# A four-layer cross-attention chain: new orders on all engines, work taken from VectorE, layer 3's maximum subtracted by VectorE, and the first feed-forward products split into three F32R products

## The reference, cut to what matters

```
L0: q,k,v = x@Wq+bq, ctx@Wk+bk, ctx@Wv+bv      16 heads of 8; causal mask (key < query), row 0 gives 0
    x = LN(x + softmax(q k^T/sqrt 8) v @ Wo + bo);  x = LN(x + relu(x@W1+b1)@W2 + b2)
L1: same attention without mask or LN;           x = x + gelu(x@W1+b1)@W2 + b2
L2: vis = mean(ctx)@Wv^T+bv; t = x@Wt^T+bt; agreement = sum(t*vis)
    r = softmax over the 64 tokens of 2*agreement
    gate = sigmoid(t@Wgt^T + (r*vis)@Wgv^T + bg);  x = LN(x + gate*r*vis)*gamma + beta
L3: n = x*rsqrt(mean x^2 + eps)*norm_w; q,k,v = n@wq, ctx@wk, ctx@wv    16 heads of 64
    out = x + softmax(q k^T) v @ wo
```

## Time and profile before

| | us |
|---|---|
| median of 3 runs | 1492.05 (1490.93 to 1493.82) |
| the profiled execution | 1493.37 |
| its span, first to last instruction | 1491.8 |
| mean granted TensorE clock, share of full speed | 0.993 |
| PE busy | 1399.8 (94%) |
| PEld busy | 1031.9 (69%) |
| DVE busy | 1074.7 (72%) |
| ACT busy | 955.0 (64%) |
| POOL busy | 504.2 (34%) |

### The profile page before, as it was taken

How to read it: one execution, slowest core, us unless ns; L and a number is a source line. 1 busy time by engine, 2 the same in 40 slices (tenths; PEclk the granted TensorE clock), 3 DMA queues, 4 the chain that set the end, 5 groups by cost and what they waited for, 6 DMA issues and landing times.

```text
span 1491.8 us, 48987 instructions
## 1 busy us (share of the span) xinstructions
PE 1399.8 (94%) x20359; PEld 1031.9 (69%) x20359; DVE 1074.7 (72%) x2647; ACT 955.0 (64%) x1879; POOL 504.2 (34%) x539
## 2 busy tenths in 40 slices
PE   5689999999999999999999999999999999999887
PEld 4356767767676676767767776776767767686666
DVE  6467778676776867778676777867678686776743
ACT  4365657576666756767576676757667676666645
POOL 3141524224251332514224251432425233251412
PEclk9899999999999999999999999999999999999999
DMA  4000000000000000000000000000000000000000
GB/s 144 15 2 2 17 9 17 9 16 10 2 17 9 17 9 2 17 9 17 9 16 10 1 18 8 17 9 8 18 1 17 9 16 10 1 10 2 2 9 9
DMA packets 27799, 20.03 MB, mean 13 GB/s; under 512 B 1088, under 2 KB 27200, under 8 KB 27328
## 3 DMA queue, kind: packets, MB, share of 16 engines
q1 hardware_dynamic: 27584, 16.90, 3.9%
HBM read 12.70 MB, written 4.19 MB: 11 GB/s over the span
## 4 chain that ended last, share of the span: by engine, by line
PE 79%; ACT 7%; DVE 6%; POOL 4%; issue 4%; DMA 0%; SPq 0%; POOLq 0%; DVEq 0%; ACTq 0%
PE bank L751 65%; PE bank L760 14%; ACT V L1114 2%; POOL prob L1202 2%; ACT prob L1132 2%; POOL prob L1182 1%; ACT K L1109 1%; DVE sums L1465 1%; DVE negmax L1311 1%; DVE z L1376 1%; POOL rstd L1189 0%; ACT probT L1064 0%; ACT room L1091 0%; DVE stats L1361 0%; DVE sums L1316 0%
## 5 line engine op out<-in xcount | busy, mean ns | idle before, releaser
L1182 POOL TENSOR_TENSOR prob<-prob,rinv 128x512 f32<-128x512 f32 x256 | 262.0, 1047 | 357.3 <-DVE rinv L1318 357.1
L760 PE MATMUL bank<-cst,prob 128*128 128x128 f32 x1536 | 213.7, 277 | 15.1 <-POOL prob L1182 7.1
L760 PEld LDWEIGHTS bank<-cst,prob 128*128 128x128 f32 x1536 | 174.3, 141 | 66.3 <-issue 37.5
L1202 POOL TENSOR_TENSOR prob<-prob,rinv 128x512 f32<-128x512 f32 x128 | 132.0, 1042 | 199.5 <-DVE rinv L1469 199.5
L1311 DVE TENSOR_REDUCE negmax<-bank 128x8 bf16<-128x512 f32 x256 | 161.3, 681 | 41.8 <-PE bank L751 41.1
L1064 ACT ACTIVATE probT<-bank 128x512 f32<-128x512 f32 x256 | 138.5, 599 | 75.0 <-PE bank L760 74.7
L1057 ACT ACTIVATE prob<-bank 128x512 f32<-128x512 f32 x256 | 141.0, 612 | 70.1 <-PE bank L751 70.0
L1316 DVE TENSOR_REDUCE sums<-prob 128x8 f32<-128x512 f32 x256 | 167.3, 653 | 17.8 <-ACT prob L1057 16.9
L1186 POOL TENSOR_TENSOR var_eps<-mv,ln_eps 128x4 f32<-128x4 f32 x48 | 15.1, 314 | 384.3 <-DVE mv L1366 384.3
L1132 ACT ACTIVATE prob<-bank,rms_rows 128x256 f32<-128x256 f32 x256 | 102.7, 481 | 46.4 <-PE bank L751 46.4
L751 PE MATMUL bank<-negmax,ident_b 128*128 128x512 bf16 x384 | 124.3, 383 | 6.4 <-DVE negmax L1311 5.1
(11 more groups left out here) (168 smaller groups left out, 2952.1 us busy)
## 6 DMA issues: line engine op xcount, KB each, us to landing
x_in<-in_x SPq DMA_DIRECT2D x16, 256.0 KB, 3.0
c_in<-in_ctx SPq DMA_DIRECT2D x16, 256.0 KB, 3.8
out<-y SPq DMA_DIRECT2D x16, 256.0 KB, 2.3
Q<-in_split_weights SPq DMA_DIRECT2D x1, 1536.0 KB, 8.4
wt<-in_weights SPq DMA_DIRECT2D x1, 1024.0 KB, 10.6
wt<-in_weights SPq DMA_DIRECT2D x1, 640.0 KB, 5.4
wt<-in_weights SPq DMA_DIRECT2D x4, 128.0 KB, 10.4
cst<-in_constants SPq DMA_DIRECT2D x1, 229.0 KB, 2.7
```

Of the source, the lines that this page charges most:

```text
L760: last = nc.tensor.transpose(o[:, k * P:(k + 1) * P], src(k), ident)
L1182: nc.gpsimd.tensor_tensor(pr, pr, ri, ALU.mult).then_inc(norm_ready.sem, 1)
L1202: nc.gpsimd.tensor_tensor(pr, pr, ri, ALU.mult).then_inc(norm3_ready.sem, 1)
```

## The change

1. `h` products: W1 of both layers moves from the F32 weights to the split ones, and `h.l.j` becomes three F32R products. Two steps a group and layer are new: `xhi` (ScalarE writes the high half `h_high`, for layer 0 from the bank of `lnF.0` once more, for layer 1 from `x2T`) and `xlo` (GpSimd, `h_low` = value minus high half). The h products wait for `xlo`.
2. Layer 3's shift: `shift3` on TensorE is gone. `sub3.m.e` on VectorE adds the negated maxima to the bank and writes the result to `prob3` in SBUF. `exp3` reads and writes `prob3` in place. The bank is free after `sub3`. The maxima are kept in F32.
3. VectorE's other work: `km` goes to ScalarE as two activations. `vm` copies 256 elements of each partition instead of multiplying 512 by a mask (the zeros are written once at the start). `agree` is gone: `ag` becomes eight products of 64 tokens, whose weights are the sequence's `gv` column repeated 128 times.
4. All four tables, the banks and `TURN` are new, with `km`, `xhi`, `xlo` and `sub3` in their places. `TURN` goes from 89.4057 to 90.4543. It only sets how the lists of the groups are merged.
5. Some waits are joined (`O` waits once for the latest `probT`, `S3.0` for all K3 and Q3 at once). The high and low halves of W1 are made at the start, one activation and one subtraction of 128x1024 more.

```diff
-SPLIT = {"Wk0": 0, "Wk1": 128, "wk3": 256, "wv3": 1280, "wq3": 2304}
+SPLIT = {"Wk0": 0, "Wk1": 128, "wk3": 256, "wv3": 1280, "wq3": 2304, "W1_0": 3328, "W1_1": 3840}
...
-TURN = 89.4057
+TURN = 90.4543
...
-            "S3": lambda g, m, e: exp3_ready(g, m, e), "PT3": lambda g, m, h: prob3T_ready(g, m, h),
+            "S3": lambda g, m, e: shifted3(g, m, e), "PT3": lambda g, m, h: prob3T_ready(g, m, h),
...
-                    pe.wait_ge(*(ln_out(g, 0) if l == 0 else attout_ready(g, 1)))
-                    mm(bank(g, "h", l, j)[:, :], w(f"W1_{l}", j * P), (x1T[0] if l == 0 else x2T)[:, :])\
+                    pe.wait_ge(*h_low_ready(g, l))
+                    split_mm(bank(g, "h", l, j)[:, :], w_split(f"W1_{l}", j * P), (h_high[:, :], h_low[:, :]))\
...
-                    mm(bank(g, "ag")[:, :], ones[:, :], agree_in).then_inc(ag_filled.sem, 1)
+                    for b in range(GB):
+                        rows = slice(b * L, b * L + L)
+                        last = mm(bank(g, "ag")[:, rows], gv[:, cg, 1, b:b + 1].broadcast_to([P, P]), x1T[1][:, rows],
+                                  start=(b == 0))
...
-                elif kind == "shift3":
-                    pe.wait_ge(*max3_ready(g, m, e))
-                    mm(bank(g, "S3", m, e)[:, :], ident_b[:, :],
-                       negmax3[:, m % 2, e, :].unsqueeze(2).broadcast_to([P, 8, L]), start=False)\
...
+                elif kind == "km":
+                    act.wait_ge(*k_filled(g, l))
...
+                    for k in range(2):
+                        last = nc.scalar.activation(Km[l][:, :, k, :], bank(g, "k", l)[:, :].rearrange("p (b k) -> p b k", b=GB),
+                                                    ACT.Identity, bias=bkm[:, l, k:k + 1], scale=m_c2[:, k:k + 1])
...
+                elif kind == "xhi":
+                    if l == 0:
+                        act.wait_ge(*lnF_filled(g, 0))
+                        nc.scalar.activation(h_high[:, :], bank(g, "lnF", 0)[:, :], ACT.Identity, bias=v("ln1_b"),
+                                             scale=v("ln1_g")).then_inc(h_high_ready.sem, 1)
+                    else:
+                        act.wait_ge(*attout_ready(g, 1))
+                        nc.scalar.activation(h_high[:, :], x2T[:, :], ACT.Identity).then_inc(h_high_ready.sem, 1)
...
+                        own = prob3[:, m % 2, :, i, :].rearrange("p (t e) k -> p t e k", e=2)[:, :, e, :]
+                        last = nc.scalar.activation(own, own, ACT.Exp, scale=rms_rows[:, 2 * m + i:2 * m + i + 1])
...
+                elif kind == "xlo":
+                    nc.gpsimd.tensor_tensor(h_low[:, :], (x1T[0] if l == 0 else x2T)[:, :], h_high[:, :], ALU.subtract)\
...
+                        last = nc.vector.tensor_copy(own[:, :, :, k, :], both[:, :, :, k, :])
...
+                elif kind == "sub3":
+                    dve.wait_ge(*max3_ready(g, m, e))
+                    own = prob3[:, m % 2].rearrange("p (t e) i k -> p e i t k", e=2)[:, e]
+                    nc.vector.tensor_tensor(own, bank(g, "S3", m, e)[:, :].rearrange("p (i t k) -> p i t k", i=2, t=4),
+                                            negmax3[:, m % 2, e, :].rearrange("p (i t) -> p i t", i=2).unsqueeze(3)
+                                            .broadcast_to([P, 2, 4, L]), ALU.add).then_inc(shifted3.sem, 1)
```

698 lines of the change are left out of this document (362 added, 336 removed).

## The result

The changed kernel takes 1526.15 us, the median of its runs (1524.46 to 1527.98), against 1492.05: a ratio of 1.023, with a 95% interval of 1.0209 to 1.0251. The forecast was 1510 with a range to 1526. The direction was right. The forecast loss was about half of the measured one (18 of 34 us), and the time lies 0.15 us above the upper end of the range.

The account below looks back on a forecast made before the run. TensorE was taken as the bound, with waits on trips through other engines. Per group -2.1 issue, +2.8 opening, +0.7 before h.0.0 gave +1.4, discounted to 15 us; plus 3 at the end: 1510 us, range 1464 to 1526.

Parts of the forecast that it names:

- The issue time: TensorE's issue per group: h products -1.2 us, layer 3 shifts -1.8, ag +0.9, in sum -2.1.
- Rival (d): By the busy table, split h products add 0.3 us each, 38 us in all: 1530 or more; chance 1%.
- The bounds of the sum: Bounds on TensorE's summed issue change over 16 groups, put at -34 us: -59 to -26.
- The way to `h.0.0`: Layer 1's first h product waits for xlo on GpSimd: +0.7 us a group (0.4 to 1.4).
- Rival (c): GpSimd's xlo, blocked by VectorE, ends up to 0.68 us later: another 0.7 a group, +11 us, 1521; chance 13%.
- The opening after: Opening of layer 3 in the changed kernel: S3.3 starts 13.3 us after the end of S3.0, against 11.85 before.
- The end of layer 3: Last group's layer 3 has nothing beside it, each pair one or two sub3 longer: +3 us.
- The conversion of W1: At the start, converting W1 falls where TensorE waits for transfers anyway: 0 to +3 us.
- I take 0.9 to 1.0, 15 us: Loss per group, cut from the summed +1.4 because some waits elsewhere would disappear; 15 us in all.
- the opening, +2.8 of waiting: Opening of layer 3: TensorE waits 4.7 us against 1.9, +2.8 a group (bounds +1.2 to +3.5).
- The place of the wait: In layer 3's opening, TensorE waits 2.6 us before PT3.0.0, with S.1.0 laid beside the trip as 1.0 us.
- the sign that was to show the forecast right: TensorE's wait for norm3 before PT3.0.0 and PT3.0.1 grows from some tenths to 2 to 3 us a group.

Follow-up runs that it names:

- e4: Changed kernel with the h products as single F32 products again, without xhi, xlo and the W1 conversion; 1532.3 us, ratio 1.0284.
- e1: Changed kernel with xT of group 1 moved on TensorE from fifth step to just before cT of group 1; 1516.7 us, ratio 1.017.
- e7: Changed kernel with group 1's xT and cT later on TensorE, its xT later on VectorE, two GpSimd weight subtractions behind norms; 1518.7 us, ratio 1.0183.
- e10: e7 with three weight conversions on ScalarE behind km.0 instead of qm.0, and VectorE's xT.0 ahead of c_low.0; 1513.0 us, ratio 1.0144.
- e2: Changed kernel with the next group's exp.0.0.0 moved on ScalarE ahead of the exponentials of layer 3's first pair; 1544.2 us, ratio 1.0359.
- e8: e7 with, in the last group, k3.6 and k3.7 later on TensorE and yn_low ahead of y_gamma and y_beta on VectorE; 1519.3 us, ratio 1.0187.
- e5: Kernel before with only sub3 on VectorE in place of shift3, behind each pair of maxima; 1549.4 us, ratio 1.0386.
- e9: Kernel before with only km moved from VectorE to ScalarE; 1536.6 us, ratio 1.0306.
- e11: e10 with layer 3's opening reordered in groups 2 to 11: shift.0.0.0 and its exponential earlier, qm.1 later; 1529.0 us, ratio 1.026.

## Why the prediction was wrong

**Read right.**
- The issue time. One split h product takes 0.70 from start to start (0.71 forecast), one `ag` step 1.83 (1.76), one `sub3` 0.56 to 0.60 where two follow each other, with 0.66 a record (0.64). Busy time would have said the contrary, and e4 confirms the sign: the split of h gains 6 to 8 us. Rival (d) is out. The bounds of the sum, -59 to -26, do not follow from those of its terms, which give -66 to -30; nothing hung on it.
- The way to `h.0.0`: 0.53 of waiting at `q.0` and 0.15 at `h.0.0`, together the 0.7 forecast. But the 0.53 is a wait for VectorE's `xT`, at a step to which the forecast gave no wait, and it is there without the split too (e4). GpSimd's rows in group 11:

```profile
1037.38 1.01 POOL L1244 TENSOR_TENSOR rstd<-var_eps,half 128x4 f32<-128x4 f32 x1
1038.42 1.29 POOL L1236 TENSOR_TENSOR h_low<-x1T,h_high 128x512 fp32r<-128x512 f32 x1
```

- Rival (c), an `xlo` blocked by VectorE, did not happen. It takes 1281 ns on average for layer 0 and 1273 for layer 1, about as long as an `xb`. But this does not test the rule behind the rival, because its condition hardly arose: 31 of the 32 `xlo` have beside them only VectorE instructions that read a bank. The one that meets an instruction on two SBUF tiles began first, and then VectorE was the one that lost: `y_beta` took 1.77 us where the fifteen others took about 0.69.

```profile
1395.00 1.77 DVE L1471 TENSOR_TENSOR y<-y,beta 128x512 f32<-128x512 f32 x1
1394.92 1.30 POOL L1236 TENSOR_TENSOR h_low<-x1T,h_high 128x512 fp32r<-128x512 f32 x1 [2.23 <-ACT h_high L1115]
```

  The Trainium skill, "SBUF — State Buffer", section "SBUF: two separate sides", says that GpSimd and VectorE share a port pair as an exclusive lock: an instruction that begins first holds it to its end, on VectorE's side one in a two-port mode or one with two SBUF inputs, the latter only against a GpSimd instruction that reads SBUF. These two rows agree with it.
- The opening after: forecast 13.3 from the end of `S3.0`, 14.4 with `S3.0` itself, measured 14.54 to 14.61 in the groups without a fall of the clock. The links agree as well: in group 10, counted from 1056.54, `PT3.0.0` starts at 6.7 (6.4 forecast), `PT3.0.1` at 8.1 (7.8) and `S3.3` at 13.4 (13.3).
- The end of layer 3: +3, as forecast.

**The steps that failed.**
1. "The conversion of W1 falls in the start, where TensorE waits for transfers anyway: 0 to +3." It was +17, half of the whole loss and the largest error of the sum; with 0 to 3 in its place the time would have lain inside the range. The sentence looked at the work that was added and not at the order in which the start was now written. For that work alone it was right: e4, without the conversion, has its first `S.0.0` 2.4 earlier. The list of TensorE's first steps showed `xT` of group 1 in fifth place, and that step needs a load that waits for `xb.0`, which waits for GpSimd's subtractions. The prediction counted the moved steps of a middle group, and of the start only the new work. e1, e7 and e10 show the three links, and with all of them mended nothing of the 17 is left at `S.0.1`, and 13 us come off the time.
2. "I take 0.9 to 1.0, 15 us" for the groups, from a sum of +1.4. Measured +0.3 a group, 3.4 us from group 2 to group 13. Two terms were off. The first is the opening, +2.8 of waiting, which with its share of the issue time is 13.3 - 11.85 = 1.45 of length. The length did grow by 1.5 on average (13.62 to 15.11), but that is luck: without falls of the clock it is 14.56, so the trips account for 0.9 and the falls for the rest. The opening before was read from a single group, 12.94, where the mean over twelve is 13.62. TensorE's waits over 0.15 us in the opening went from 1.6 to 3.0 a group, +1.4 where +2.8 was forecast. The second is how much comes back elsewhere. The group less its opening is 75.3 us before and 74.1 after, -1.2, where the forecast's terms give -0.1 and its discount -0.5. Half of that difference is the split of h: the forecast charged it with 0.7 of waiting, and it waits 0.15, so it gains 1.1 and not 0.5. In which steps the other half came back no run has told. Against it stand the falls of the clock, for which the prediction had nothing: about 1 us each. With two of them and not six, as in e1 and e7, there is no loss in the middle at all.
3. The place of the wait. `S.1.0` was laid beside the trip as 1.0 us of work that waits for nothing. Its fourth bank was not looked up. In the length of the opening it did no harm, since the wait there and the trip to `PT3.0.0` run side by side, as e2 shows. But the sign that was to show the forecast right, a wait for GpSimd of 2 to 3 us in front of the first two `PT3`, did not appear: it is 0.76 us in group 10. Nor did the wait of 0.5 to 1 us for `h_low`.
4. "+3 us at the end." Layer 3 was right, and the 8 us ahead of it were not looked for. Read from the traces, 4 fall before `o.1` of the last group, 1 between that and `lnT.2`, 3 in the q3 products at half clock and the wait for `yn_low`. Why they fall there was not settled: e8, the one run on it, changed nothing.

The errors partly cancel: 17 and 11 us where 0 to 3 and 3 were forecast, and 3.4 where it was 15, beside 3 between the first scores and group 2. The upper end of the range was loose as well: the prediction gives its own case 1528 in the sum and 1520 in the chances, and 1526 for the whole, and only the first holds the 1526.15. A sum nearer to the truth would not have meant that the terms were right.

## What to carry to other kernels

When a change rewrites an order, lay the first and the last steps of the program side by side with the old ones, as carefully as those of a middle round: a step that a transfer feeds, moved to the front, costs its wait once. Here the start was half the loss. Read both sides of a difference over all repetitions, not from one. In a schedule fitted this closely, a part taken alone (e5, e9: +58 and +45 us) or a move made by reasoning at one place (e2, e11: +16 to +18) costs more than the terms say, most likely because waits elsewhere were cut to the old durations. The runs show the cost outside the touched place (e5, e11), not its reason.

## What the runs showed of the hardware

- TensorE's granted clock fell from 2.4 to 1.2 GHz around single waits of 1.9 to 3.1 us, in a kernel where it was busy for over 90% of the time. In the changed kernel and in e1 the fall came between half a us before the end of the wait and 3 us behind it. Before, with waits of some tenths in the same place and none over 1.71 us, it did not fall once in 1340 us. The same wait did not always do it: the groups 2 to 12 have eleven waits of 2.28 to 2.38 us, and the clock fell at six of them in the changed kernel and at two in e1. What decides stays open.
- A VectorE instruction on two SBUF tiles that began 0.07 us after a GpSimd instruction on SBUF took 1.77 us and not 0.69, about as if it had waited for the end of the other. The same pair of steps shows it in e1 and e10 as well (1.77). The other way round, the kernel before has `rstd` at 1.01 us in 34 of 48 cases and at about 1.45 in 14, each of these beside VectorE's `x2T`, an instruction on two SBUF tiles.
- A copy of half as many elements was not half as long: `Vm` took 416 ns for 256 elements, against 681 for 512 with a mask. In-place exponentials on SBUF took 506 ns against 481 from PSUM.
